# Run-length attention: in which step a turned block of exponentials leaves its PSUM bank

## The reference, cut to what matters

```python
a = einsum('bthd,bshd->bhts', iq, ik)         # scores of softmaxed q and k
y[r, c] = a[r, c] * (y[r-1, c-1] + 1)         # run length along each diagonal, r >= c
x = y + c / (r + 1)                           # and masked above the diagonal
o = softmax(x / 0.1, axis=-1) @ iv            # then times the per-head output matrix
```

## Time and profile before

| | |
|---|---|
| runs | 1615.15, 1606.83, 1610.93 us, median 1610.93 |
| the profiled execution | 1611.11 us, of which the span of instructions is 1609.4 |
| the stage `rosa_attention` | first scan at 259.4 us, last operation at 552.6 |
| busy in the whole span | PE 1183.4 us (74%), PEld 960.6 (60%), DVE 928.7 (58%), ACT 676.1 (42%), POOL 595.8 (37%) |
| granted TensorE clock, whole span | 0.859 of full speed |

### The profile page before, as it was taken

One profiled execution on the slowest core, in us unless ns is written; L12 is line 12 of the kernel. 1 busy time (PEld: TensorE's weight loads), 2 busy tenths in 40 slices (PEclk: granted clock), 3 DMA queues, 4 the chain that ended last, 5 costly groups with the idle time before them and its releaser, 6 DMA issues. The chain is left out here.

```text
span 1609.4 us, 30797 instructions
## 1 busy us (share of the span) xinstructions
PE 1183.4 (74%) x8969; PEld 960.6 (60%) x9000; DVE 928.7 (58%) x2702; ACT 676.1 (42%) x1493; POOL 595.8 (37%) x705
## 2 busy tenths in 40 slices
PE   4468869888977656749999927899999740079992
PEld 3367434545666544449999925677777640078991
DVE  7654986625687355325555548776767550056774
ACT  3422745645555324436666612333333310055651
POOL 5500340355645205723434322021112007746660
PEclk9679989999999757869999967999999755589995
DMA  2279011000000251111111121000000201112225
GB/s 71 52 118 155 16 41 26 13 12 8 9 2 2 80 236 46 53 38 47 49 46 47 44 81 40 1 1 0 0 0 0 85 34 53 53 49 60 65 59 162
DMA packets 91143, 78.60 MB, mean 49 GB/s; under 512 B 21808, under 2 KB 84016, under 8 KB 89776
## 3 DMA queue, kind: packets, MB, share of 16 engines
q1 hardware_dynamic: 81072, 56.98, 13.7%
q0 software_dynamic: 9984, 20.53, 3.8%
HBM read 44.29 MB, written 33.18 MB: 48 GB/s over the span
## 5 line engine op out<-in xcount | busy, mean ns | idle before, releaser
L1785 PE MATMUL m_eps_up<-m_ext,m_w_up 128*128 128x128 f32 x1856 | 238.2, 279 | 1.1 <-DVE m_w_up L1832 0.7
L1751 POOL DMA_INDIRECT ys_scratch<-m_yout,m_xin x152 | 159.1, 1047 | 204.1 <-DVE m_yout L1853 149.4
L1785 PEld LDWEIGHTS m_eps_up<-m_ext,m_w_up 128*128 128x128 f32 x1856 | 222.2, 194 | 4.4 <-issue 2.0
L1806 ACT ACTIVATE m_w_up<-m_up 128x512 f32 x152 | 95.8, 630 | 193.5 <-PEq L1578 142.2
L1606 POOL DMA_INDIRECT xs_scratch<-m_xn,m_slot x128 | 122.8, 959 | 114.9 <-POOLq L1373 44.1
L1795 PE MATMUL m_eps_y<-m_w_down,m_ht 128*128 128x128 f32 x1216 | 161.4, 276 | 0.6 <-DVE m_ht L1845 0.5
L1795 PEld LDWEIGHTS m_eps_y<-m_w_down,m_ht 128*128 128x128 f32 x1216 | 148.7, 193 | 1.0 <-DVE m_ht L1845 0.7
L1775 PE MATMUL m_eps_x<-ident,m_xin 128*128 128x128 f32 x152 | 44.1, 291 | 139.6 <-DMA m_xin<-xs_scratch 139.2
L2060 POOL TENSOR_TENSOR c_kx<-c_k,head 128x2048 f32<-128x2048 f32 x16 | 57.6, 3603 | 229.4 <-ACT c_k L2083 229.4
L2087 ACT ACTIVATE c_e<-c_e 128x512 f32<-128x512 f32 x96 | 60.4, 630 | 187.3 <-DVE c_e L2136 187.3
L1826 DVE COPY m_ext<-m_eps_x 128x128 f32<-128x128 f32 x152 | 42.7, 281 | 129.3 <-PE m_eps_x L1775 126.9
(11 more groups left out here) (317 smaller groups left out, 2607.1 us busy)
## 6 DMA issues: line engine op xcount, KB each, us to landing
xs_scratch<-empty SPq DMA_DIRECT2D x20, 516.0 KB, 11.1
m_xin<-xs_scratch SPq DMA_DIRECT2D x152, 64.5 KB, 1.8
m_y<-ys_scratch SPq DMA_DIRECT2D x22, 256.0 KB, 5.2
m_up<-in_m_gate SPq DMA_DIRECT2D x2, 2048.0 KB, 14.4
m_up<-in_m_up SPq DMA_DIRECT2D x2, 2048.0 KB, 19.2
m_down<-in_m_down SPq DMA_DIRECT2D x2, 2048.0 KB, 23.7
a_q_in<-q_scratch SPq DMA_DIRECT2D x80, 32.0 KB, 1.7
c_rows<-ys_scratch SPq DMA_DIRECT2D x10, 256.0 KB, 3.1
```

What stands on the lines that cost most here:

```text
L1751: pool.indirect_dma_start(ys_dram, bass.IndirectOffsetOnAxis(xin[:, u, C:C + 1].bitcast(U32), 0), yout[:, u, :], None).then_inc(stored[u], 16)
L1785: last = pe.matmul(ps[u % 2][:, k * P:(k + 1) * P], w[:, u % 2, k * P:(k + 1) * P], xt[:, u % 2, :], start=True, stop=True)
L1806: act.activation(w_up[0][:, u % 2, :], m.up[0][:, e, :], ACT.Copy).then_inc(placed[0], 1)
```

## The change

The block that `turn_back` wrote leaves its bank one step earlier (BACK 3 to 2), on ScalarE and VectorE alike. On ScalarE it is moved within the step too: behind the drain and the copies of scores, ahead of the exponential. Since `sums_at` uses BACK, the eight sums of each of the first three quarters move one step earlier as well (steps 2 to 9 of the following quarter), and two groups instead of three are left for after the loop. TensorE's and GpSimd's code is unchanged but for that.

```diff
-BACK = 3
+BACK = 2
...
             for g in range(NGROUP):
-                if g >= BACK:
-                    back(g - BACK)
                 for q, m in sums_at(g):
                     drain(q, m)
                 for n in units_at(g):
                     for k in units[n][3]:
                         hold(n, k)
+                if g >= BACK:
+                    back(g - BACK)
                 exp(g)
```

## The result

| | before | changed |
|---|---|---|
| median of 5 runs | 1610.93 us (1605.12 to 1615.15) | 1619.06 us (1618.47 to 1625.28) |
| ratio, 95% interval | | 1.0064 [1.0032, 1.0095] |
| profiled execution, span | 1611.11, 1609.4 | 1619.06, 1617.4 |
| `rosa_attention`, first scan to last count | 293.2 | 301.0 |

What follows compares the result with a forecast made beforehand. The stage was taken as bound by loops of engines waiting on each other, with TensorE the chain in steps 35 to 42. The terms summed to +10.0, the clock -1, on 1611.1: 1620 us, range 1611 to 1627.

Steps and rivals of the forecast that it cites:

- quarters 0 and 1, with the clock's -2: First two quarters: +0.3 us in quarter 0, 0 in quarter 1, and -2 for one of three lower-clock stretches gone.
- steps 34 to 42: Quarter 2 steps with sums and scores: a loop through TensorE and VectorE closes within one step, together +9.4 us.
- steps 43 to 49, with the clock's +1: Plain steps gain 1.1 us, step 43 loses 2.0, copies cost 0.4: +1.3; new idle time may bring lower clock, +1.
- steps 50 to 57: Quarter 3 steps with sums, no scores: a new loop through VectorE takes 9.7 against 9.05 us for two steps, +2.0.
- steps 58 to 62: Plain steps of quarter 3: turn to scan gets shorter, -0.18 us each, -1.0 in all.
- after the loop: One block fewer before the end: copies and a turn's wait go, -2.5 us; VectorE's `back` ahead of last maxima +0.5; -2.0.
- near 1: Sign against the prediction: granted clock near 1 from 305 to 385 us, where it averaged 0.91 before.
- The tie within one step: Quarter 2, steps with sums: turn, `back`, count, scans, scale, weigh, scores, turn; 5.95 and 7.85 us against 4.53 and 6.43.
- Rival 2: Whole stage: VectorE's tie to TensorE's current step doesn't matter, only gains remain, 18.7 us, giving 1592 us; chance 0.05.
- The 1.0 late spreads of quarter 0: Quarter 0, steps 3, 9 and 13: spreads now follow the turn, each 1.0 us late, +3.1 against 2.8 gained.
- net 0: Quarter 1: 3.4 us gained at drain waits, lost again to scans and sums waiting in steps 17, 21 and 29.
- rival 1: Quarter 1's three drain waits no longer let the clock fall: a further -6 us, 1614 to 1615 us; chance 0.20.

## Why the prediction was right, point by point

The time (1620 forecast, 1619.06 measured), the sign and the cause of the loss were right. How near the time came is partly luck: the terms are up to 1.6 us off, and those errors cancel in part. The sizes by term, with the two parts of the clock where the prediction expected them:

| term | forecast | measured |
|---|---|---|
| quarters 0 and 1, with the clock's -2 | -1.7 | -2.7 |
| steps 34 to 42 | +9.4 | +9.5 |
| steps 43 to 49, with the clock's +1 | +2.3 | +3.6 |
| steps 50 to 57 | +2.0 | +0.9 |
| steps 58 to 62 | -1.0 | -2.6 |
| after the loop | -2.0 | -1.2 |
| sum | +9.0 | +7.7 before rounding (span +8.0) |

The signs that the prediction named came too, with one exception: VectorE waits for the turn in nearly every step, TensorE before L1080 for the scale, 18.0 us of TensorE's wait are left, the long drain waits are 1.09 shorter each, and the tail is 2.53 shorter. The exception is the clock: "near 1" between 305 and 385 us was to mean that the prediction is wrong, and it is 0.98. By that sign the prediction of the clock was wrong: the lower stretches went further than it took. The loops, which make the sign of the result, came as forecast.

- **The tie within one step** (steps 34 to 42). Right in the mechanism and in the size: 5.95 and 7.85 forecast, 5.99 to 6.06 and 7.85 to 7.96 measured in the sums with count. The wait of TensorE before L1080 is 1.37 to 1.46 (1.4 forecast) and starts at 0.93 where there is no count. Taking VectorE's `back` a step later in these steps takes 9.8 us off, the whole +9.5; taking the count out of the loop gives 0.4 a step. Rival 2 is shown wrong by both. It would have been right of ScalarE's half alone.
- **Quarters 0 and 1.** The 1.0 late spreads of quarter 0 came (TensorE waits 0.94 for L990), and the gain at the copies too (2.21 became 1.13): +1.5 in place of +0.3. ScalarE's half alone takes 42.9 there, the whole change 47.5, so VectorE's tie cost 4.6 in quarter 0, where 3.1 was forecast. In quarter 1 the drain waits are 2.18, 2.34 and 2.42, where before they were 3.27, 3.43 and 3.51; only one has lower clock behind it (324.1 to 327.5), and it is the first, the shortest:

```profile
322.93 1.09 PE L1093 MATMUL a_ps_o<-ident,a_os 128*64 128x128 f32 x8 [2.18 <-ACT a_os L1155]
```

  Before, 13.6 us from group 16 to 34 ran at the lower clock (0.92 over 83.8 us); now 3.4. The 10.2 us that are gone held up to 5 us of excess, which is the size of the -4.2, with the "net 0" beside it; this split wasn't tested by itself. The prediction took one stretch of three to be gone; it was two. This is rival 1's mechanism, and its condition (two of three stretches stay away) was met; it did not decide the sign, because at most about 5 us came of it, less than the 6 that rival 1 took, and step 43 gave 1.7 back. The Trainium skill, TensorE: Matmul & The Clock Gate, "HAM oscillation — how this bites in real kernels", has it that work after such waits starts at the lower level. The trace agrees in part. A lower stretch came with each of the three long waits of before, but at the first two the turned sums behind the wait still ran at full clock (1.09) and the level fell 1.6 and 1.2 us after they had started (320.5 and 347.8); only the third found it fallen (1.97). Of the three shorter waits one has a lower stretch.
- **Steps 43 to 49: step 43 mis-sized.** Step 43 was put at 6.9; it took 9.15. (Before the change it took 4.56, where the prediction had 4.9; the other six steps together gave -0.95, where -0.7 was forecast.) The changed kernel in that step, timeline:

```profile
444.24 1.34 POOL L1293 TENSOR_TENSOR a_z<-a_y,a_peak 128x688 f32<-128x688 f32 x1
...
446.29 0.58 ACT L1132 ACTIVATE a_held<-a_ps_score 128x512 f32<-128x512 f32 x1
...
447.02 2.04 PE L1027 MATMUL a_ps_score<-a_qx,k_t 128*128 128x512 f32 x2 [2.58 <-ACT a_held L1132]
...
448.86 1.80 PE L1054 MATMUL a_ps_back<-ident,a_z 128*128 128x128 f32 x8
...
450.69 0.69 DVE L1215 TENSOR_TENSOR a_held<-a_ps_back,a_factor 128x512 f32<-128x512 f32 x1 [6.07 <-PE a_ps_back L1054]
```

  The chain is the one of the prediction (exponential, copy behind it, second score, turn, VectorE), but the second score and the turn run at half clock after a wait of 2.58, 2.04 and 1.80 in place of 1.10 and 1.04: 1.7 more. The window of that stretch:

```profile
447.00:450.40 3.40, 3.38 (x10) 2.26 (x11) 0.00 (x0) 1.05 (x3) 0.00 (x0) 0.50 0.00 0
```

  The remaining 0.5 lies ahead of the exponential: from the scan (442.54) to the copy behind it (446.29) are 3.75, where 3.2 was taken. The maxima end at 443.64, and GpSimd centres at 444.24, since two spreads (442.19, 2.10 us) stand ahead; the prediction left GpSimd out of this step. With the count ahead of `back` step 43 took 7.09. That this is near 6.9 is partly chance, for the count's 0.4 is gone from it and GpSimd's 0.5 is in it. But it shows the clock's part by itself. The same score stands there behind the same wait, and at full clock:

```profile
454.15 1.10 PE L1029 MATMUL a_ps_score<-a_qx,k_t 128*128 128x512 f32 x2 [2.58 <-ACT a_held L1134]
```

  From the score's start to VectorE's `back` it is 1.7 us less than in the changed kernel. The mechanism was right; the clock, which the prediction had put at +1 for steps 34 to 43, and GpSimd were the rest.
- **Steps 50 to 57.** 9.2 to 9.4 for two steps where the sum gave 9.6 to 9.7 (and 9.0 to 9.2 before). The first term was too long: turned sums to turn is 3.21 (489.32 to 492.53), not 3.39. In the 3.39 of rows 7, 0.18 lie between weigh and turn, most likely a wait for the bank, which ScalarE was emptying until 491.77 and which the earlier `back` leaves free by then. What the rest is, isn't settled. TensorE in the changed kernel:

```profile
489.32 1.09 PE L1093 MATMUL a_ps_score<-ident,a_os 128*64 128x128 f32 x8
...
492.53 1.09 PE L1054 MATMUL a_ps_back<-ident,a_z 128*128 128x128 f32 x8
```

- **Steps 58 to 62** (first scans of groups 59 to 63). Of the -2.6, 2.0 lie in steps 61 and 62: 4.90 and 4.51 before, 3.72 and 3.72 now. Before, 6.8 us there ran at the lower level (0.82 over 17.4 us); the changed kernel runs all of it at 1.00 up to 527.1. So most of the gain is most likely the clock, which the prediction did not count here. Another 0.7 is the last scale of quarter 2's sums, which stood in step 59 (4.45) and now stands in step 58, counted in the stretch before. Step 60, without either, takes 3.51 before and 3.65 now, so that the forecast 0.18 a step isn't seen there.
- **After the loop.** Last exponential to first weigh took 5.12 (535.01 to 540.13 below) where before it took 7.65, 2.53 less and just what was forecast (2.5). But the way to that exponential, from the first scan of group 63, is 1.37 longer (7.87 for 6.50), where I gave 0.5: the turn ran at half clock (1.94, before 1.06), VectorE's `back` waited 1.29 for it, and the last maxima queued behind. The changed kernel's timeline:

```profile
529.21 1.94 PE L1054 MATMUL a_ps_back<-ident,a_z 128*128 128x128 f32 x8 [2.71 <-ACT a_held L1147]
...
531.18 0.69 DVE L1215 TENSOR_TENSOR a_held<-a_ps_back,a_factor 128x512 f32<-128x512 f32 x1 [1.29 <-PE a_ps_back L1054]
...
531.79 1.21 DVE L1204 TENSOR_REDUCE a_peak<-a_y 128x4 f32<-128x1024 f32 x1
...
535.01 1.06 ACT L1162 ACTIVATE a_z<-a_z 128x1024 f32<-128x1024 f32 x1 [2.16 <-POOL a_z L1293]
...
540.13 1.94 PE L1080 MATMUL a_ps_o<-a_held,vp 128*32 128x64 f32 x64 [0.83 <-ACT a_held L1147]
```

- **What was not foreseen at all:** how good ScalarE's half is alone. The prediction gave 18.7 us for the case that VectorE's tie cost nothing; it is 23.6. (The 18.7 counts 14 plain steps, and by its own list there are 12: 17.7.) The largest part of what was missed lies in quarters 0 and 1: 9.8 us, where 2.8 and 3.4 were taken.

The Trainium skill's rule under Perfetto Trace Analysis, "Optimization Strategy" (find the busiest engine's waits, make what they wait for start sooner), was shown half right: the version that does that for ScalarE alone takes TensorE's wait from 25.1 to 7.4 us and 1.3% off the time, and the whole change takes it to 18.0 and adds 0.6%, since it moves a second engine's half that no wait asked for.

## What to carry to other kernels

Before a consumer is moved a step earlier, name the producer's place in that step and everything that queues behind the consumer: if a turn stands late in the producer's step, the consumer should be a step behind, and costs nothing there as long as its bank isn't the one that is waited for. Where one constant moves two engines, split it and try the halves: here they were worth 24 us less and 95 us more on their own. And an operation moved behind others within its step may need the step earlier as well, or it closes a loop (31 us here).

## What the runs showed of the hardware

The granted clock follows waits of a few us less regularly than the prediction took it. Before, TensorE's waits of 3.27 to 3.51 in quarter 1 each had a lower stretch with them. In the changed kernel the wait of 2.18 there has one and those of 2.34 and 2.42 have none; and before, 2.21 in quarter 0 had none. The wait of 2.58 in step 43 has one, and with the count ahead of `back` the same wait ahead of the same score has none. With ScalarE's new order alone, three of eight waits of 1.93 had one. So between 1.9 and 2.6 the length of the wait doesn't tell by itself. What the lower level costs can be read in step 43: the same second score takes 2.04 instead of 1.10 us, the same turn 1.80 instead of 1.04.

The same kernel before took 1610 to 1611 us beside some runs and 1661 and 1662 on other chips, 3% more. Of those chips there is no trace of the kernel before, but in the traces of the other kernels a scan, a turn or a score of this stage takes as long as here, and all of the 50 us lie outside the stage.
